# Two scan states added on GpSimd or VectorE ahead of TensorE's summing matmuls, in batches 2 to 6 of a fused Mamba, gate and attention kernel

## The reference, cut to what matters

```python
delta = jax.nn.softplus(dbc[..., :dt_rank] @ dt_proj_w + dt_proj_b)
A = -jnp.exp(A_log)
deltaA = jnp.exp(delta[..., None] * A)
BX = (delta * xc)[..., None] * Bm[:, :, None, :]
def step(h, inp):
    dA, bx, c = inp
    h = dA * h + bx
    return (h, jnp.einsum('ben,bn->be', h, c))
...
y = jnp.swapaxes(ys, 0, 1) + D_param * xc
y = y * jax.nn.silu(z)
return y @ out_proj_w
```

## Time and profile before

| what | value |
|---|---|
| three runs | 1682.96, 1522.29, 1521.08 us; median 1522.29 |
| profiled execution | 1525.04 us, span 1523.3 us, mean granted TensorE clock 0.952 |
| busy over the span | PE 90%, PEld 44%, DVE 74%, ACT 56%, POOL 42% |
| first stage, one iteration (330.3 to 409.0 us) | 78.7 us: PE 78.0 busy, DVE 71.95, POOL 64.21, ACT 55.88 |

### The profile page before, as it was taken

The page is one execution under the profiler, slowest core; times in us unless marked ns, Lnnn a source line. Parts: engine busy times, 40 slices in busy tenths (PEclk is TensorE's granted clock), DMA queues, the critical chain, the costliest instruction groups (busy, mean ns, idle before and its releaser), DMA issues.

```text
span 1523.3 us, 17326 instructions
## 1 busy us (share of the span) xinstructions
PE 1365.3 (90%) x5574; PEld 664.6 (44%) x5574; DVE 1129.6 (74%) x1814; ACT 857.9 (56%) x1488; POOL 646.1 (42%) x387
## 2 busy tenths in 40 slices
PE   6427799999999998999858889999999999999998
PEld 2103445454545555555422334444445454444444
DVE  4889888989899898931278877786868777776335
ACT  6656676767676764531104656556565656555633
POOL 2596969797969685723033212213130222100000
PEclk9757999999999999999957999999999999999999
DMA  4843443434343433012073333343232433330145
GB/s 139 285 143 112 127 151 130 139 134 138 137 137 96 160 139 112 28 42 69 25 168 85 91 79 78 78 98 85 59 96 59 98 72 68 72 71 3 35 143 170
DMA packets 93802, 158.04 MB, mean 104 GB/s; under 512 B 8608, under 2 KB 74720, under 8 KB 90592
## 3 DMA queue, kind: packets, MB, share of 16 engines
q1 hardware_dynamic: 93712, 156.94, 35.7%
HBM read 110.91 MB, written 46.01 MB: 103 GB/s over the span
## 4 chain that ended last, share of the span: by engine, by line
PE 61%; DVE 15%; issue 10%; POOL 6%; ACT 5%; DMA 2%; SPq 0%; POOLq 0%; ACTq 0%; DVEq 0%
PE psum L1070 23%; PE psum L2055 8%; PE psum L1989 7%; PE psum L1963 6%; PE psum L1978 5%; DVE mx L1452 5%; PE psum L1933 4%; DVE psum L566 3%; PE psum L1122 2%; POOL hb L1003 2%; PE psum L1095 1%; DVE middle L549 1%; DVE stats L1428 1%; ACT back L796 1%; PE psum L2150 1%
## 5 line engine op out<-in xcount | busy, mean ns | idle before, releaser
L1703 ACT ACTIVATE pw<-psum 128x512 f32<-128x512 f32 x512 | 302.1, 598 | 274.3 <-PE psum L1978 270.9
L1452 DVE TENSOR_REDUCE mx<-psum 128x1 f32<-128x512 f32 x512 | 344.0, 686 | 151.7 <-PE psum L1963 150.5
L1003 POOL TENSOR_TENSOR hb<-ddb,bcb 128x1024 f32<-128x1024 f32 x127 | 296.6, 2359 | 69.0 <-DVE middle L549 54.5
L566 DVE TENSOR_TENSOR_SCAN psum<-psum,hb 128x512 f32<-128x512 f32 x224 | 261.6, 1213 | 22.9 <-POOL hb L1003 12.2
L1963 PE MATMUL psum<-kp,qp 96*128 96x512 bf16 x512 | 203.6, 403 | 33.0 <-DVE mx L1452 21.6
L792 ACT ACTIVATE psum<-ddb,A_neg 128x512 f32<-128x512 f32 x256 | 165.4, 682 | 84.0 <-DVE hb L569 67.1
L1978 PE MATMUL psum<-qp,kp 99*128 99x512 bf16 x512 | 197.6, 387 | 5.0 <-ACT pw L1703 4.3
L1871 POOL TENSOR_TENSOR rstd<-rstd,neg_half 128x4 f32<-128x4 f32 x16 | 16.3, 1017 | 415.2 <-DVE rstd L1437 415.2
L569 DVE TENSOR_TENSOR hb<-psum,bcb 128x1024 f32<-128x1024 f32 x112 | 137.2, 1225 | 3.9
L1989 PE MATMUL psum<-pw,v_sb 128*32 128x512 f32 x1024 | 124.3, 602 | 0.5 <-ACT pw L1703 0.5
L1070 PE MATMUL psum<-back,w 128*128 128x512 f32 x256 | 114.9, 600 | 4.0 <-ACT back L808 1.9
(11 more groups left out here) (214 smaller groups left out, 2085.2 us busy)
## 6 DMA issues: line engine op xcount, KB each, us to landing
ddb<-dd SPq DMA_DIRECT2D x64, 512.0 KB, 6.8
bcb<-bc SPq DMA_DIRECT2D x32, 512.0 KB, 6.7
parts<-parts_sb SPq DMA_DIRECT2D x96, 128.0 KB
qp<-parts SPq DMA_DIRECT2D x32, 256.0 KB, 7.8
dd<-dd_out SPq DMA_DIRECT2D x7, 1024.0 KB, 4.9
kp<-parts SPq DMA_DIRECT2D x16, 384.0 KB, 4.7
x_back<-x_dram SPq DMA_DIRECT2D x9, 512.0 KB, 8.4
xh_back<-xh SPq DMA_DIRECT2D x8, 512.0 KB, 3.8
```

What stands on the lines that cost most here:

```text
L566: e.tensor_tensor_scan(to[:, g, :], a[:, g, :], h[:, g, :], 0.0, ALU.mult, ALU.add).then_inc(scan_ok, 1)
L1003: e.tensor_tensor(hb[n % NHB], ddb[k % NSLOT][:, 1:2, :].to_broadcast([P, 2, L]), bcb[q][:, 0, :, :], ALU.mult).then_inc(bx_ok, 2 if n == ...
L1452: used.up(e.tensor_reduce(mx[u % 2][:, n:n + 1], score_bank(used.n), AXIS.X, ALU.max))
L1703: e.activation(pw[n % NPW], bank(5 + n % 2), ACT.Exp, scale=HD ** -0.5).then_inc(exp_ok, 1)
```

## The change: what it does

For batches 2 to 6, in groups 1 and 3 of a batch's four groups, the two states of a partition are added into the first one, in place, before TensorE sums. GpSimd does this addition (`add_states`, 128x512 float32) for units 4, 5, 6, 7 and 12; VectorE does it for units 13, 14 and 15, right after its multiplication by C, with a wait for that multiplication. TensorE then needs four matmuls instead of eight for such a group, and waits for two further semaphores, `add_pool` and, in group 3, `add_dve`.

```diff
+        def added(b, group):
+            return 2 <= b < NB - 1 and group % 2 == 1
...
                     e.tensor_tensor(h, a, bcb[q][:, 1, :, :], ALU.mult).then_inc(hc_dve, 1)
+                    if added(b, u // 4) and u >= 12:
+                        e.wait_ge(hc_dve, dve_hc(n))
+                        e.tensor_tensor(h[:, 0, :], h[:, 0, :], h[:, 1, :], ALU.add).then_inc(add_dve, 1)
...
+            def add_states(b, u):
+                n = NUNIT * b + u
+                if u in POOL_HC:
+                    e.wait_ge(hc_pool, len(POOL_HC) * b + POOL_HC.index(u) + 1)
+                else:
+                    e.wait_ge(hc_dve, dve_hc(n))
+                h = hb[n % NHB]
+                e.tensor_tensor(h[:, 0, :], h[:, 0, :], h[:, 1, :], ALU.add).then_inc(add_pool, 1)
...
                     if u == 6 and front:
                         front_power(i + 2)
+                    if s and 6 <= u <= 8 and added(i, 1):
+                        add_states(i, u - 1)
                     if s and u in POOL_HC:
                         hC(i, u)
+                        if added(i, u // 4):
+                            add_states(i, u)
...
-                for g in range(2):
+                ng = 2
+                if added(b, group):
+                    ng = 1
+                    e.wait_ge(add_pool, 5 * (b - 2) + (4 if group == 1 else 5))
+                    if group == 3:
+                        e.wait_ge(add_dve, 3 * (b - 1))
+                for g in range(ng):
                     for jj in range(4):
                         h = hb[(NUNIT * b + 4 * group + jj) % NHB]
                         ins = e.matmul(bank(4)[jj * EB:(jj + 1) * EB, :], sel, h[:, g, :], start=(q == 0 and g == 0),
-                                       stop=(q == 1 and g == 1))
+                                       stop=(q == 1 and g == ng - 1))
```

More of the change, by code:

```diff
@@ L296, in build @@
         bc_sent, bc_in = [sem(f"bc_sent{i}") for i in range(2)], [sem(f"bc_in{i}") for i in range(2)]
+        add_dve, add_pool = sem("add_dve"), sem("add_pool")
         dd_sent, dd_in = sem("dd_sent"), [sem(f"dd_in{i}") for i in range(NSLOT)]
```

## The result

1554.66 us median against 1524.47 us of the kernel before, run beside it on the same chip (four runs each): ratio 1.0206, 95% interval 1.0188 to 1.0224, so +31.4 us by the ratio. One of the four runs of the kernel before was a slow one (1682.96 us), which the ratio leaves out but the median does not: by medians the difference is +30.2 us, without that run +32.4 us (1522.29 us before). The change makes the kernel about 2% slower; whether a little over or under 2% the interval leaves open. The forecast was 1552 us; its sum was +30.

A forecast was written before the change was run, and what follows sets the result against it. TensorE bounds from 298 to just short of 358 us, then VectorE until the next norm. Per iteration 5.4 - 0.93 + 2.1 + 0.4 = +7.0, four times +28, plus 2.2 for batch 6: +30, 1552 us, range 1540 to 1568.

The forecast's parts named there:

- stall ahead of sums 1: TensorE, reaching sums 1 at 314.52 us, waits until 319.9 for GpSimd's addition of unit 7: 5.4 us per iteration.
- halved sums 1: TensorE's group 1 sums, on the chain, lose half their 16 records: 0.93 us saved per iteration.
- clock: TensorE behind the stall at sums 1: granted clock falls to the lower level, costing 2.1 us, ends 0 and 3.0.
- group 3 and the port: Unit 15's VectorE addition waits for a GpSimd instruction; gate state 0.6 us late, about 0.4 us lost per iteration.
- batch 6, all: Iteration of batch 6, without front work: 2.5 us stall, -0.93 and +0.6 for the late gate state, +2.2 us.
- 3.04 us idle stretch: Profile row where TensorE's next product ran at full speed; batch 6's 2.5 us stall, being shorter, should leave the clock up.
- second rival: TensorE's clock stays up over the stall at sums 1: 4 x 2.1 us less, 1544 us; 12%.
- first rival: GpSimd keeps the port over gapless instructions, delaying additions of units 14 and 15: +44 us on top, 1596 us; 14%.
- Third rival: TensorE does not wait at sums 1; ten halved groups count, 5 x 0.93 and 5 x 0.13 us: 1517 us; 3%.
- slack of 0.13 us at the back sum: VectorE is ready 0.13 us before TensorE's product releases it; only 0.13 of group 3's 0.93 us reaches the end.
- wait for TensorE in back_new: On VectorE, this wait covers the additions of units 13 and 14, 0.69 us each, 0.73 with the dependence.
- fourth rival: Narrow fit of front sum, last decays and bx 15 fails; unit 15 late by 2 us or more: 1560 us and over; 6%.

The follow-up runs named there:

- e4: Changed kernel plus five throwaway matmuls on TensorE ahead of the wait at sums 1 in batches 2 to 5: 1552.0 us, ratio 1.0187 to the kernel before.
- e5: Changed kernel with TensorE doing gate gc ahead of sums 1 in batches 2 to 6: 1552.15 us, ratio 1.0192 to the kernel before.
- e7: Changed kernel, group 1 alone, VectorE adding units 5 to 7 from two SBUF inputs, ScalarE's relu 4 and 5 ahead of decay 9: 1528.31 us, ratio 1.0033.
- e3: Changed kernel with matmuls of groups 1 and 3 halved but no addition made or waited for: 1520.37 us, ratio 0.9985 to the kernel before.
- e1: Changed kernel with only group 3 halved, group 1 summed as in the kernel before: 1529.52 us, ratio 1.0041 to the kernel before.
- e9: Changed kernel with gate gc ahead of sums 1 and only group 1 halved, its additions on GpSimd: 1529.89 us, ratio 1.0047 to the kernel before.
- e2: Changed kernel with only group 1 halved, all four additions on GpSimd: 1555.36 us, ratio 1.0211 to the kernel before.

## Why the prediction was right, point by point

**The sum.** +30 was forecast, +31.4 measured by the ratio, and 29.6 in the trace from sums 2 of batch 1 to sums 2 of batch 7. Its terms, per iteration of batches 2 to 5, counted from start to start so that nothing falls between the records. Sums 1 and sums 2 of the kernel before, batch 3:

```profile
314.45 1.92 PE L1122 MATMUL psum<-hb,sel 128*32 128x512 f32 x16
...
330.28 1.92 PE L1122 MATMUL psum<-hb,sel 128*32 128x512 f32 x16
```

The first starts 0.07 us ahead of the 314.52 of the chain; the table goes by the records.

| term | forecast | measured | from |
|---|---|---|---|
| stall ahead of sums 1 | +5.4 | +5.5 | norm to sums 1: 29.25 us (296.83 to 326.08) against 23.73 before (290.72 to 314.45) |
| halved sums 1 | -0.93 | -0.86 | sums 1 to sums 2: 14.97 in e4 against 15.83 before |
| clock | +2.1 | +1.6, twice +2.0 | 16.61, twice 17.00, against 14.97 |
| group 3 and the port | +0.4 | +0.2 | a remainder: what is left of 85.2 - 78.7 = 6.5 in batch 3 |
| batch 6, all | +2.2 | +1.9, and +1.2 behind it | iteration 80.6 against 78.7, the next one 75.8 against 74.7 |

**The stall** came at its place, by its releaser and with its size. The working held because both ends were counted from one common start, the norm, and the addition's price, interpolated between 2.36 and 0.20 us, was 1.28 us against a measured 1.26 to 1.28. Of the 5.5 us TensorE spends 0.46 and 4.70 idle in two pieces (the rest is the end of the record ahead of each). The first piece is its wait for a relu behind decay 9, which waits for unit 7's product and so for bx 7: the same lateness of GpSimd by another way, not seen in the prediction and swallowed by the larger stall.

**The clock** fell in all four iterations, not in batch 6 (1.79 us of idle time there; 2.5 was forecast). For batch 6 the prediction leant on the 3.04 us idle stretch that had left the clock up. That row is no bound: in e5 the clock fell behind a wait of 2.48 us (granted 0.67 from 351.94 to 357.17 us) and stayed up behind one of 2.46 us in the next iteration (1.00 from 436.41 on). The length of the wait alone does not decide it. The second rival, a clock that stays up, is out by the 3.27 us of four products and the granted clock of 0.59. Its price as a rival was wrong, though: e4 shows that with the clock up the iteration is 84.5, not the 83.6 that 85.2 less 1.6 would be, so it would have given about 1552, not 1544.

**The port** behaves as the prediction took it from the earlier trace rows: an addition with two SBUF inputs waits for the end of the GpSimd instruction that is running. It takes 1.35 to 1.84 us at the three places in the changed kernel, 2.74 (the median) in e7, where two of the three meet GpSimd's densest stretches, and 0.69 as soon as one input is in PSUM. The Trainium skill's rule (SBUF — State Buffer, section "SBUF: two separate sides") agrees: turns for whole instructions, no sharing of bandwidth. The first rival, that GpSimd keeps the port over instructions in a row, is excluded by e7: the longest of 15 additions, in stretches of up to three multiplications, took 2.87 us. That page of the Trainium skill has the loser blocked for one whole instruction and says nothing of a run of them; here it was one.

**Third rival.** Its condition did not come about (the wait is there). Without the wait the halved groups would win at most what e3 shows, 2 to 4 us (ratio 0.9985), less than the 5.3 that the rival's working gives.

**Where the working failed without the number showing it.** Three places. First, group 3. The prediction read a slack of 0.13 us at the back sum and gave 0.13 of the 0.93 us; in e3 the whole of group 3's gain goes into TensorE's wait for the bank that the gate state frees, which the step did not look for. The changed kernel has the same wait, four times 0.9 us. Second, the wait for TensorE in back_new that was to cover the additions of units 13 and 14: e1 shows that it does not, since the two additions meet GpSimd's multiplications and put 3.2 us ahead of a wait of 2.77. In the changed kernel it was covered all the same, but by the stall. Third, and most: the sum treats the stall as the path and all else as hidden beside it. e4 and e5 show that a second path, GpSimd's stream through bx 13 into VectorE, ends only some 0.7 us earlier. The number was right because the longer of the two was the one that was summed, by 0.7 us that nobody had reckoned; there the forecast had luck. Anyone who had used the same working to mend the kernel, by moving TensorE's sums, would have expected next to nothing left of the 30 us, and got +29 (e5).

**The fourth rival** (unit 15 late by the front sum) did not happen in the changed kernel, where VectorE waits for TensorE instead (0.65 us, in back_new). In e9, without the stall, it does: VectorE's scan of unit 15 waits 0.61 us for ScalarE's decay, and TensorE 1.9 us for that unit.

## What to carry to other kernels

An instruction put into a dense stream delays all that is behind it, and the first consumer to stall hides the others: after finding the stall, ask what the iteration would be without it (here 84.5 instead of 85.2). Before halving a step, leave its work out altogether: that run gave the ceiling, 2 to 4 us, of which group 3 had none. Additions that cost next to nothing while the engine that makes them has waits to spare cost their whole length once another change has used those waits (0.8 us alone, 4.0 behind a late GpSimd). And when a gain is right on one engine but does not arrive, look for sub-microsecond waits that another engine's written order hands on; here two moves on ScalarE turned 1.000 into 0.9974.

## What the runs showed of the hardware that was not expected

- VectorE's addition beside GpSimd's stream: 0.69 us with one input in PSUM, median 2.74 with both in SBUF, and GpSimd loses too (7.43 us for three multiplications instead of 7.01). Three instructions with one SBUF input each (0.70 + 0.68 + 0.69 us) are cheaper beside that stream than a product and an addition from SBUF (1.22 + 2.74).
- A group of eight sums behind a stall of 4.7 us took 1.94 us at the lower clock in e2, 1.94, 1.44, 1.30 and 1.94 in the four iterations of the changed kernel after the same idle time, and 1.06 at full clock. Against the 14.97 us at full clock, the stretch from sums 1 to sums 2 was longer by 1.6 to 2.3 us in the stalled iterations of the two kernels. How long a wait was does not say by itself whether the clock falls: 2.48 us in one iteration of e5 brought it down, 2.46 us in the next did not.
